# First stage of a metaformer kernel: the reciprocal standard deviations go to DRAM as all 32 rows and come back by one transfer of 128 partitions per norm

## The chip, the cores and the metric

The kernel runs on one core of a Trainium2 chip. The metric is the device time of one execution in microseconds (us).

## What is computed

The input x has the shape (2, 64, 256, 256): 2 images, 64 channels, 65,536 pixels each. The reference, cut to its skeleton:

```python
x = x + _L0_conv_ref(_ln_c(x), L0_conv_kernel)                  # norm over channels, 3x3 depthwise convolution
t = _to_tokens(x)
t = t + _L0_ffn_ref(_ln_t(t), W, V, gamma, beta)                # norm over channels, W, batch norm, recurrence with sigmoid
x = _from_tokens(t, x)
x = x + _L1_conv_ref(_ln_c(x), ...)                             # norm, linear attention
t = t + _L1_ffn_ref(_ln_t(t), ...)                              # norm, experts with top-8 tokens
```

The norms take mean and variance over the 64 channels of each pixel:

```python
def _ln_c(v, eps=1e-06):
    m = jnp.mean(v, axis=1, keepdims=True)
    s = jnp.var(v, axis=1, keepdims=True)
    return (v - m) / jnp.sqrt(s + eps)
```

The first stage of the kernel holds the first norm, the convolution with its addition (giving x1), the second norm, the product with W (giving u) and the sums for the batch norm. The change is in this stage alone.

## The kernel before

**Tiles.** The 2 x 64 channels of the two images lie on the 128 partitions: image b on partitions 64b to 64b + 63. The pixels run along the free dimension, in 32 blocks (NBLK) of 2048 pixels (BLOCK, 8 KB per partition), each of 4 tiles of 512 pixels (TILE, TPB = 4). A block of x is 1 MB.

**Order.** Each engine has its own program, written out by hand as a loop over steps t, one tile per step. At step t an engine does the work of tile t - lag for each kind of work; the lags are constants (CENTER 5, TAPS 8, SUMS 9, FINISH 10, PROJECT 22, SCALE 23). Waits are on semaphores. A round n of statistics comes every 4 steps and serves two norms at once: the first norm of block n (l = 0) and the second norm of block n - 4 (l = 1, BEHIND = 4 rounds). There are 36 rounds; rounds 0 to 3 hold only the first norm, rounds 32 to 35 only the second.

**A round.** TensorE multiplies the tiles and their squares with stat_of, which puts the mean of image b for norm l and tile j of the block into 8 equal rows of PSUM: partitions 32j + 16l + 8b to 32j + 16l + 8b + 7. VectorE takes the squared mean away (line 623), ScalarE makes 1/sqrt by a logarithm and an exponential (lines 501, 505, 509). The result is the tile `rstd` of 128 partitions x 512: 4 tiles x 2 norms x 2 images x 8 equal copies.

**The way to the channels.** A norm needs rstd on all 64 channels of an image. SyncE does it through DRAM. `rstd_to_dram(n)` (line 360) writes one of the 8 copies: for each norm and image one transfer of 4 rows of 2 KB, 8 KB in all. `rstd_to_channels(l, k)` (line 369) waits until these have landed and reads the 8 KB row of an image back into 64 partitions, one transfer of 512 KB per image, two per norm. The second norm's wait for the written rows is left out where the first norm of the same round has waited already. The tile `rb[l]` holds two blocks; it is overwritten when VectorE has used the block two before. The profile names rb[0] and u together with x as `arena`, rb[1] as `rstd_wide`.

**SyncE's order in a step**: write rstd (t - 2), spread rstd (t - 3), store x1 (`x_scratch<-arena`, line 376), store u (`xl_scratch<-arena`, line 380), load x six tiles ahead (`arena<-in_x`, line 354). All these transfers share the queue q1. After block 27's projections SyncE also issues the loads of region 0 for the second stage (`first_regions`, line 132); region 1 follows when the last u is stored.

**Users.** VectorE multiplies the centered tile with rstd of the first norm in `norm_x` (line 594, halo rows in 591 and 593), adds taps of the convolution (line 617), and multiplies the projected tile with rstd of the second norm in `scale_wx` (line 634), which also waits for the store of u two blocks before. ScalarE makes products of taps and squares, GpSimd adds them up (lines 559, 566).

**After the stage.** The sums of u give the batch norm (line 667 on), and the second stage runs the recurrence over the regions of u (first matmuls at line 859).

Of the kernel before, what the change touches and what calls it, by code (L numbers as in the profile page):

```python
# [15 lines left out]
B, C, H, W = 2, 64, 256, 256  # L16
P = B * C
N = H * W
TILE = 512
# [49 lines left out]
def build_program(nc, x, conv_k, ffn_w, ffn_v, gamma, beta, q_w, q_b, kv_w, kv_b, proj_w, proj_b,  # L69
# [4 lines left out]
    with stack:  # L74
# [6 lines left out]
        def dram(name, shape, dt=F32):  # L81
            return nc.dram_tensor(name, shape, dt, kind="Internal").ap()
# [138 lines left out]
        with ExitStack() as ph:  # L221
# [29 lines left out]
            psw = [ph.enter_context(nc.psum_tensor(f"psw{j}", [P, TILE], F32)) for j in range(2)]  # L251
            rstd_d = [dram(f"rstd_scratch{l}", (NBLK, B, BLOCK)) for l in range(2)]

# [21 lines left out]
            STEPS_A = NT + SCALE + 6  # L275

            def round_of(l, k):
                return k + BEHIND * l
# [5 lines left out]
            def rstd_written(n):  # L284

                return rstd_out[n % 2], sum(16 * B * len(norms_in(m)) for m in range(n % 2, n + 1, 2))

# [58 lines left out]
            def _(sp):  # L346
# [9 lines left out]
                def rstd_to_dram(n):  # L356
                    sp.wait_ge(rstd_ready, n + 1)
                    for l, k in norms_in(n):
                        for b in range(B):
                            sp.dma_start(rstd_d[l][k, b, :].rearrange("(j n) -> j n", n=TILE),  # L360
                                         rstd[16 * l + 8 * b:P:32, n % 2, :]).then_inc(rstd_out[n % 2], 16)

                def rstd_to_channels(l, k):
                    if l == 0 or k >= NBLK - BEHIND:
                        sp.wait_ge(*rstd_written(round_of(l, k)))
                    if k >= 2:
                        sp.wait_ge((normed, u_ready)[l], TPB * (k - 1))
                    for b in range(B):
                        sp.dma_start(rb[l][b * C:(b + 1) * C, k % 2, :],
                                     rstd_d[l][k, b, :].partition_broadcast(C)).then_inc(rb_loaded[l][k % 2], 16)  # L370

# [205 lines left out]
            def _(dve):  # L577
                dve.wait_ge(pads_ready, 1)

                def norm_x(g):  # L580
                    k, q = g // TPB, g % RT
                    dve.wait_ge(centered, g + 1)
                    dve.wait_ge(rb_loaded[0][k % 2], 32 * (k // 2 + 1))
                    if g >= RT:
# [40 lines left out]
                def scale_wx(g):  # L625
                    k = g // TPB
                    dve.wait_ge(wx_ready, g + 1)
                    dve.wait_ge(rb_loaded[1][k % 2], 32 * (k // 2 + 1))
                    if g % TPB == 0 and 2 <= k < NBLK - 2:
# [1357 lines left out]
```

## Time and profile before

| what | value |
|---|---|
| time, median of 3 runs | 1800.78 us (1798.41 to 1800.98) |
| profiled execution | 1805.67 us |
| its span, first to last instruction | 1803.9 us |
| busy in the span | TensorE 79%, VectorE 77%, ScalarE 68%, GpSimd 77% |
| first stage | about 20 to 681 us of the span |
| transfers of rstd to DRAM in the stage | 128, 8 KB each |
| transfers of rstd to the channels in the stage | 128, 512 KB each |

The span is the time from the first to the last instruction of one profiled execution. In the rows below PE is TensorE, PEld its weight loads, DVE VectorE, ACT ScalarE, POOL GpSimd, SP SyncE, SPq what SyncE's queue issues; L369 is line 369. The DMA share is the mean busy share of the core's 16 DMA engines. Busy times are of one execution; an idle time in brackets names what ended it.

### The profile page before, as it was taken

How to read it: one execution, taken by the hardware profiler on the slowest of the kernel's cores; microseconds unless marked ns; L12 is line 12 of the kernel's file. 1: busy time of each engine (PE TensorE's matmuls, PEld its weight loads, DVE VectorE, ACT ScalarE, POOL GpSimd, SP SyncE). 2: the span in 40 equal slices, each digit the busy share in tenths (PEclk: the TensorE clock that was granted, in tenths of full speed). 3: DMA queues.
4: the chain of work that ended last, by engine and by line, in shares of the span. 5: the costliest groups of instructions: out<-in, count | busy, mean ns of one | idle time of the engine just before them, and what ended most of it. 6: DMA issues, size and time to landing. Idle time of an engine off the chain costs nothing. (4 is left out here: it accounts for less than half of the span.)

```text
span 1803.9 us, 23731 instructions
## 1 busy us (share of the span) xinstructions
PE 1430.1 (79%) x5369; PEld 589.3 (33%) x5369; DVE 1384.6 (77%) x2395; ACT 1220.0 (68%) x2320; POOL 1398.0 (77%) x1029
## 2 busy tenths in 40 slices
PE   3889999999999956999926789999999999816100
PEld 1233333333333313666613333333333333205100
DVE  1899999999999954999935469999999999941000
ACT  2678888878788755999923488898898898610000
POOL 2899999999999930588882099999999999801575
PEclk8999999999999987999976899999999999955555
DMA  4579999999999889499975258988898887660011
GB/s 128 160 211 289 276 289 275 289 278 281 288 272 289 227 278 394 162 423 425 405 290 233 48 171 267 292 291 269 287 294 272 283 294 220 205 163 7 1 2 2
DMA packets 111403, 429.77 MB, mean 238 GB/s; under 512 B 44672, under 2 KB 47648, under 8 KB 66208
## 3 DMA queue, kind: packets, MB, share of 16 engines
q1 hardware_dynamic: 91376, 423.77, 73.0%
q10 hardware_dynamic: 16432, 4.29, 1.4%
q8 instruction: 47, 0.77, 0.2%
q0 software_dynamic: 3456, 0.19, 0.2%
q14 instruction: 92, 0.75, 0.1%
HBM read 257.89 MB, written 170.01 MB: 237 GB/s over the span
## 5 line engine op out<-in xcount | busy, mean ns | idle before, releaser
L617 DVE SCALAR_TENSOR_TENSOR pst<-xn,kk,pst 128x512 f32<-128x512 f32 x448 | 336.3, 751 | 7.8 <-PE pst L449 1.6
L449 PE MATMUL pst<-xn,taps 128*128 128x512 f32 x512 | 243.8, 598 | 44.6 <-DVE acc L617 44.6
L559 POOL TENSOR_TENSOR x_and_products<-tap_products,x_and_products 128x512 f32<-128x512 f32 x192 | 245.1, 1277 | 30.1 <-ACT tap_products L527 2.7
L1528 POOL TENSOR_SCALAR exp_q<-exp_q 128x512 f32<-128x512 f32 x128 | 189.6, 1481 | 75.7 <-ACT exp_q L1479 75.7
L527 ACT ACTIVATE tap_products<-xn,kk 128x512 f32<-128x512 f32 x320 | 214.9, 710 | 28.7 <-POOL x_and_products L559 25.1
L1523 POOL TENSOR_TENSOR sq_norm<-arena 128x512 f32<-128x512 f32 x128 | 188.7, 1474 | 4.4 <-DVE arena L1575 1.7
L559 POOL TENSOR_TENSOR x_and_products<-tap_products,arena 128x512 f32<-128x512 f32 x128 | 163.5, 1277 | 22.8 <-ACT tap_products L527 22.7
L945 DVE SCALAR_TENSOR_TENSOR pss<-arena,bn,pss 128x256 f32<-128x256 f32 x324 | 149.6, 489 | 32.9 <-PE pss L859 32.5
L566 POOL TENSOR_TENSOR arena<-acc,x_and_products 128x512 f32<-128x512 f32 x128 | 163.8, 1280 | 9.1 <-DVE acc L617 8.3
L1535 POOL TENSOR_TENSOR q_z<-arena,z_inv 128x512 f32<-128x512 f32 x128 | 165.4, 1292 | 0.0
L489 ACT ACTIVATE sq<-arena 128x512 f32<-128x512 f32 x256 | 146.4, 615 | 23.6 <-DMA arena<-in_x 21.6
L449 PEld LDWEIGHTS pst<-xn,taps 128*128 128x128 f32 x512 | 93.6, 189 | 180.4 <-issue 178.9
L1412 PE MATMUL ps_denominator<-arena,dT 128*128 128x512 f32 x256 | 138.6, 623 | 9.9 <-DVE arena L1569 8.6
L464 PE MATMUL psw<-arena,wcT 128*128 128x512 f32 x256 | 133.1, 605 | 16.1 <-DVE arena L634 15.8
L1406 PE MATMUL ps_query<-arena,qcT 128*128 128x512 f32 x256 | 140.3, 632 | 4.7 <-DVE arena L1560 4.7
L1795 POOL DMA_INDIRECT out<-fin,word_of_slot x88 | 86.5, 983 | 71.7 <-DVE fin L1949 45.1
L458 PE MATMUL psc<-arena,cst 128*128 128x512 f32 x256 | 136.7, 617 | 5.5 <-DVE xn L594 5.5
L1485 ACT ACTIVATE ln_d<-ps_denominator,cols 128x512 f32<-128x512 f32 x128 | 86.9, 679 | 73.0 <-PE ps_denominator L1412 72.8
L1418 PE MATMUL ps_attended<-q_z,mT 128*128 128x512 f32 x256 | 130.9, 593 | 1.1 <-POOL q_z L1535 1.1
L1569 DVE SCALAR_TENSOR_TENSOR arena<-arena,q_bias_plus,exp_q 128x512 f32<-128x512 f32 x128 | 125.5, 980 | 1.8 <-POOL exp_q L1528 1.8
L1575 DVE SCALAR_TENSOR_TENSOR arena<-ps_attended,cols,arena 128x512 f32<-128x512 f32 x128 | 95.2, 744 | 38.8 <-PE ps_attended L1418 38.0
L894 POOL TENSOR_TENSOR x_block<-x_block,arena 128x2048 f32<-128x2048 f32 x20 | 111.1, 5556 | 15.9 <-ACT arena L886 9.7
(243 smaller groups left out, 2959.0 us busy)
## 6 DMA issues: line engine op xcount, KB each, us to landing
arena<-rstd_scratch SPq DMA_DIRECT2D x128, 512.0 KB, 8.5
x_scratch<-arena SPq DMA_DIRECT2D x36, 1024.0 KB, 5.0
arena<-x_scratch SPq DMA_DIRECT2D x36, 1024.0 KB, 5.3
arena<-in_x SPq DMA_DIRECT2D x32, 1024.0 KB, 8.0
rstd_wide<-rstd_scratch SPq DMA_DIRECT2D x64, 512.0 KB, 13.1
xl_scratch<-arena SPq DMA_DIRECT2D x32, 1024.0 KB, 15.6
out<-arena SPq DMA_DIRECT2D x32, 1024.0 KB, 6.6
x_transposed<-x_squares SPq DMA_DIRECT2D x64, 512.0 KB, 4.4
```

Source lines behind the costliest of these rows:

```text
L449: m = pe.matmul(wide(pst[g % 2]), taps[:, n * P:(n + 1) * P], tap_rows(g, t), start=(n == 0), stop=(n == len(mine) - 1))
L489: act.activation(sq[l][:, g % TPB, :], x_tile(g), ACT.Square).then_inc(squared[l], 1)
L527: act.activation(prod[:, q % NP, :, :], tap_rows(g, t), ACT.Copy, scale=kk[:, t:t + 1]).then_inc(products, 1)
L559: pool.tensor_tensor(xr[:, g % XR, :], prod[:, q % NP, :, :].rearrange("p r w -> p (r w)"), xr[:, g % XR, :] if n else x_tile(g), ALU.add) ...
L566: pool.tensor_tensor(x_tile(g), acc[:, g % 2, :, :].rearrange("p r w -> p (r w)"), xr[:, g % XR, :], ALU.add).then_inc(x1_ready, 1)
L617: dve.scalar_tensor_tensor(out=out, in0=tap_rows(g, t), scalar=kk[:, t:t + 1], in1=wide(pst[g % 2]), op0=ALU.mult, op1=ALU.add).then_inc(a ...
L945: dve.scalar_tensor_tensor(out=ps_at(r, j), in0=u, scalar=gain_w, in1=ps_at(r, j), op0=ALU.mult, op1=ALU.add).then_inc(summed, 1)
L1406: pe.matmul(pq[g % 2][:, :], qcT[:, :], x_tile(g), start=True, stop=True).then_inc(q_ready, 1)
L1412: pe.matmul(pd[:, :], dT[:, :], qm[:, g % QSLOTS, :], start=True, stop=True).then_inc(d_ready, 1)
L1523: pool.tensor_tensor(sq[1][:, g % SQSLOTS[1], :], x_tile(g), x_tile(g), ALU.mult).then_inc(squared[1], 1)
L1528: pool.tensor_scalar(e, e, 1.0, None, ALU.min).then_inc(clipped, 1)
L1535: pool.tensor_tensor(qz[:, g % 2, :], qm[:, g % QSLOTS, :], zr[:, g % 2, :], ALU.mult).then_inc(qz_ready, 1)
```

## The change

`rstd_to_dram` writes all 32 rows of each of the 4 partition groups, so every one of the 8 copies of both norms and images: 4 transfers of 64 KB in each round, also in the rounds with a single norm (whose other rows hold no statistics that anyone reads). `rstd_to_channels` reads a norm's 16 rows (8 copies for each image) by one transfer of 1 MB into 128 partitions, each row 8 times in a row. The scratch in DRAM becomes one tensor of 36 x 32 x 2048, and the counts of the waits follow.

```diff
-            rstd_d = [dram(f"rstd_scratch{l}", (NBLK, B, BLOCK)) for l in range(2)]
...
+            rstd_d = dram("rstd_scratch", (ROUNDS, 32, BLOCK))
...
             def rstd_written(n):
 
-                return rstd_out[n % 2], sum(16 * B * len(norms_in(m)) for m in range(n % 2, n + 1, 2))
+                return rstd_out[n % 2], 16 * TPB * (n // 2 + 1)
...
                 def rstd_to_dram(n):
                     sp.wait_ge(rstd_ready, n + 1)
-                    for l, k in norms_in(n):
-                        for b in range(B):
-                            sp.dma_start(rstd_d[l][k, b, :].rearrange("(j n) -> j n", n=TILE),
-                                         rstd[16 * l + 8 * b:P:32, n % 2, :]).then_inc(rstd_out[n % 2], 16)
+                    for j in range(TPB):
+                        sp.dma_start(rstd_d[n, :, cols_of(j)],
+                                     rstd[32 * j:32 * j + 32, n % 2, :]).then_inc(rstd_out[n % 2], 16)
 
                 def rstd_to_channels(l, k):
                     if l == 0 or k >= NBLK - BEHIND:
                         sp.wait_ge(*rstd_written(round_of(l, k)))
                     if k >= 2:
                         sp.wait_ge((normed, u_ready)[l], TPB * (k - 1))
-                    for b in range(B):
-                        sp.dma_start(rb[l][b * C:(b + 1) * C, k % 2, :],
-                                     rstd_d[l][k, b, :].partition_broadcast(C)).then_inc(rb_loaded[l][k % 2], 16)
+                    rows = rstd_d[round_of(l, k), 16 * l:16 * l + 16, :]
+                    sp.dma_start(rb[l][:, k % 2, :],
+                                 rows.unsqueeze(1).to_broadcast([16, P // 16, BLOCK])).then_inc(rb_loaded[l][k % 2], 16)
...
-                    dve.wait_ge(rb_loaded[0][k % 2], 32 * (k // 2 + 1))
+                    dve.wait_ge(rb_loaded[0][k % 2], 16 * (k // 2 + 1))
...
-                    dve.wait_ge(rb_loaded[1][k % 2], 32 * (k // 2 + 1))
+                    dve.wait_ge(rb_loaded[1][k % 2], 16 * (k // 2 + 1))
```

## Rows read from the trace of the kernel before

**Rows 1.** Busy by stretch (window, its length, busy per engine), two rounds.

```profile
core 0: us, PE busy (x) PEld busy (x) DVE busy (x) ACT busy (x) POOL busy (x), PEclk, DMA share, GB/s
147.50:165.90 18.40, 16.87 (x63) 6.42 (x63) 17.81 (x32) 15.84 (x31) 17.54 (x15) 1.00 1.00 290
...
391.20:410.00 18.80, 18.03 (x66) 7.01 (x65) 18.48 (x33) 15.38 (x31) 17.58 (x15) 1.00 0.96 277
```

**Rows 2.** Groups by line, VectorE, 100 to 640: busy, mean ns | idle before <-releasers.

```profile
L617 DVE SCALAR_TENSOR_TENSOR pst<-xn,kk,pst 128x512 f32<-128x512 f32 x403 | 302.5, 751 | 5.8 <-PE pst L449 0.6
L617 DVE SCALAR_TENSOR_TENSOR acc<-xn,kk,pst 128x512 f32<-128x512 f32 x115 | 86.0, 748 | 4.1
...
L634 DVE SCALAR_TENSOR_TENSOR arena<-psw,rstd_wide 128x512 f32<-128x512 f32 x113 | 77.3, 684 | 0.4 <-DMA xl_scratch<-arena 0.3
```

**Rows 3.** Timeline, VectorE, start: start us, us, instruction, [idle before <-releaser].

```profile
43.65 1.29 DVE L594 TENSOR_TENSOR xn<-psc,arena 128x512 f32<-128x512 f32 x2 [7.60 <-DMA arena<-rstd_scratch]
```

**Rows 4.** Timeline, VectorE, end of the stage.

```profile
666.75 0.69 DVE L634 SCALAR_TENSOR_TENSOR arena<-psw,rstd_wide 128x512 f32<-128x512 f32 x1 [10.54 <-issue]
...
676.07 0.69 DVE L634 SCALAR_TENSOR_TENSOR arena<-psw,rstd_wide 128x512 f32<-128x512 f32 x1 [4.21 <-DMA rstd_wide<-rstd_scratch]
...
680.04 0.69 DVE L634 SCALAR_TENSOR_TENSOR arena<-psw,rstd_wide 128x512 f32<-128x512 f32 x1 [1.01 <-PE psw L464]
```

**Rows 5.** Busy by stretch: x load, spread, 128-partition transfers, weights into 64.

```profile
34.50:38.00 3.50, 3.50 (x8) 1.17 (x4) 0.70 (x1) 0.00 (x0) 0.00 (x0) 0.50 0.98 328
38.50:42.00 3.50, 0.49 (x1) 0.00 (x0) 0.00 (x0) 3.30 (x6) 0.00 (x0) 0.88 1.02 225
...
1606.00:1611.00 5.00, 0.00 (x0) 0.00 (x0) 2.37 (x11) 0.00 (x0) 0.00 (x0) 0.50 1.11 199
...
646.00:657.00 11.00, 8.00 (x29) 2.18 (x28) 6.26 (x16) 8.03 (x19) 1.27 (x1) 1.00 1.02 424
```

**Rows 6.** Timeline, SyncE's queue, a late round: issue us, time of issuing, transfer.

```profile
391.20 2.33 SPq L360 DMA_DIRECT2D rstd_scratch<-rstd  x4
...
395.65 1.45 SPq L369 DMA_DIRECT2D arena<-rstd_scratch  x2
...
398.42 0.59 SPq L380 DMA_DIRECT2D xl_scratch<-arena  x1
```

**Rows 7.** Timeline, SyncE's queue, start of the stage.

```profile
32.28 1.17 SPq L360 DMA_DIRECT2D rstd_scratch<-rstd  x2
33.49 0.43 SPq L354 DMA_DIRECT2D arena<-in_x  x1
34.62 1.13 SPq L369 DMA_DIRECT2D arena<-rstd_scratch  x2
```

**Rows 8.** Timeline, SyncE's queue, end of the stage.

```profile
635.70 1.07 SPq L360 DMA_DIRECT2D rstd_scratch<-rstd  x2
...
640.62 2.71 SPq L132 DMA_DIRECT2D arena<-xl_scratch  x4
650.46 1.07 SPq L360 DMA_DIRECT2D rstd_scratch<-rstd  x2
...
658.66 1.13 SPq L369 DMA_DIRECT2D rstd_wide<-rstd_scratch  x2
...
660.46 1.37 SPq L360 DMA_DIRECT2D rstd_scratch<-rstd  x2
668.39 1.12 SPq L369 DMA_DIRECT2D rstd_wide<-rstd_scratch  x2
```

**Rows 9.** Transfers, 100 to 640: count, KB each, median us from issue to landing.

```profile
xl_scratch<-arena SPq DMA_DIRECT2D x28, 1024.0 KB, 15.7
arena<-rstd_scratch SPq DMA_DIRECT2D x54, 512.0 KB, 10.2
```

**Rows 10.** Timeline, VectorE, the round after that of rows 6.

```profile
409.63 0.68 DVE L594 TENSOR_TENSOR xn<-psc,arena 128x512 f32<-128x512 f32 x1
...
415.78 0.68 DVE L634 SCALAR_TENSOR_TENSOR arena<-psw,rstd_wide 128x512 f32<-128x512 f32 x1
```

## What I predict, and how the numbers come out of the rows

> **What bounds the kernel now.** I read the busy shares by stretch first, then VectorE's groups of instructions in the first stage, then what waited for a transfer out of the rstd scratch, and last the issues of SyncE at both ends of the stage.
>
> In the middle of the first stage VectorE is busy for 18.48 of 18.80 us of a round [rows 1]. Of the 540 us from 100 to 640 it sat idle some 10 us in front of three of its groups, and only 0.9 us of that has a releaser: 0.6 us TensorE, 0.3 us the store of u [rows 2]. So VectorE sets the pace, and the spread of rstd, which this change touches, is hidden there. But the DMA engines are nearly full too: share 0.96 in a late round, 1.00 in an early one [rows 1]. Spreads of the first stage are waited for only at its ends: block 0's, 7.60 us [rows 3], the last block's, 4.21 us, and by my reading that of the block before it: the 10.54 us that are put down to nothing end when it lands [rows 4]. Between them lies only hidden work; the change must show at these two ends, or by filling the DMA engines until they set the pace.
>
> **The price of a spread.** The load of 1 MB of x in front of block 0's spread ran at 328 GB/s with its start, and stretches of loads and stores of 128 partitions at 424 GB/s; the spread behind that load, two transfers of 64 partitions out of one 8 KB row each, ran at 225 GB/s [rows 5]. For 1.05 MB that is 2.5 us at 424 and 4.7 us at 225. A load of weights into 64 partitions, whose source is not repeated, ran at 199 GB/s [rows 5], so repeating the source is not needed for the low rate.
>
> The new spread is one transfer of 128 partitions, but with 16 rows at its source, and each row's eight copies fill eight neighbouring partitions. No row of before shows this form. Its price lies between the two above: 2.5 us (2.2 us gained) and 4.7 us (nothing gained); nothing excludes a little more. I take 4.7 us, the row nearest to it: same tile, same bytes, rows read over and over. All the 424 GB/s rows have a source row of its own for each partition.
>
> **Part by part.**
>
> Writes, rounds with one norm (the first four and the last four). Line 360 issues four transfers instead of two: 2.33 us for four [rows 6] against 1.17 for two [rows 7] and 1.07 [rows 8], so the last one is out 1.0 to 1.2 us later. All that SyncE has behind it in its order (store of x1, load of x, the wait for the written rows at line 369, spread, store of u) comes 1.0 us later.
>
> Writes, rounds with two norms. Four issues before and after, so no time on SyncE. The bytes grow from 32 to 256 KB a round: 0.6 us of all DMA engines at 424 GB/s, 1.2 us at 225 GB/s, against under 0.15 us now. I take 0.65 us, because an issue takes over 0.5 us and the transfers so come one after another [rows 6]; 1.2 us stays in the range.
>
> Spread issues. One instead of two per norm: 1.45 us for two now [rows 6]. SyncE waits for ScalarE's rstd anyway before the next round, so this is worth nothing; at most the store of u goes out up to 1.2 us earlier, into a full queue.
>
> Waits on 16 instead of 32 in VectorE's order: same place, no price. ScalarE's wait before it overwrites an rstd buffer is two rounds old when it comes.
>
> *Start of the stage.* Now: two writes at 32.28, load of x at 33.49, spread at 34.62 [rows 7], first use at 43.65 [rows 3]. After: load and spread go out 1.0 us later, the load's data is still in front, so the spread lands 1.0 us later at 4.7 us a spread (at 2.5 us: 1.0 - 2.2 = 1.2 us earlier). VectorE does nothing else there and is never idle for long afterwards, so **+1.0 us** stays.
>
> *Middle.* A round has 18.80 us; 0.96 of that is 18.05 us of DMA work, and 0.65 us more makes 18.7: it still fits, barely. How late things may come: the store of u issued at 398.42 takes 15.7 us and so lands at 414.1, and VectorE overwrites that buffer at 415.78, 1.7 us of cover; the spread for VectorE's L594 goes out in two issues from 395.65 and lands 10.2 us after the second (about 396.4), at 406.6, for 409.63, 3 us of cover [rows 6, 9, 10]. In early rounds with share 1.00 there is no room, and some four of them add 0.65 us each, 2.6 us, against that cover. I take **+1.5 us** of new stalls, from 0 to 4.
>
> *End of the stage.* Here one transfer waits for the other [rows 8]. At 635.70 two sets of rows are written; at 640.62 the four loads of region 0 (4 MB, about 10 us at 424 GB/s) go out behind the spread; the writes of 650.46 have to pass all of that and let the spread go only at 658.66; its use is at 666.75 with the next writes (660.46) behind it; these let the last spread go at 668.39, whose use is at 676.07; the last tile starts at 680.04 [rows 4, 8]. After: 1.0 us by the issues at 635.70 (the engines have nothing to do then, so all behind is moved), 0.6 us by the bytes of the writes at 650.46, 0.6 us by those at 660.46, whose extra issues hide behind the store of u. Sum **+2.2 us**. If that cover were gone, 0.5 us more. All of stage two's loads and its first matmuls follow the last tile, so nothing behind takes it back.
>
> Sum: 1.0 + 1.5 + 2.2 = 4.7 us on the span of 1803.9 (1805.67 us with what lies around it). That execution is 4.9 us (0.27%) above the median of 1800.78; I put the difference on the median: 1805.5 us. With the bounds (0 to 4 in the middle, 0.5 either way at each end): 1802.5 to 1809.
>
> **Rivals.**
>
> *The spread gets the full rate* (2.5 us). Then block 0's spread lands 1.2 us earlier. At the end: first writes' issues +1.0, spread -2.2 in front of the region loads, bytes +0.6: the second spread goes out 0.6 us earlier, lands 2.8 earlier; bytes +0.6, -2.2 again: the last lands 4.4 us earlier. The middle gains nothing but the 0.3 us of [rows 2], since VectorE sets the pace. Sum -5.9: 1795 us. It decides once a spread takes under about 3.9 us: four spreads stand on the path (one at the start, three at the end), which then return the 1.0 + 2.2 us that the writes cost. For it: 64 partitions without a repeated source are just as slow [rows 5], so the 128 could be the cure. Against it: the source's 16 rows. The Trainium skill's page SBUF — State Buffer (same section) speaks for this case.
>
> *Partly relieved*: the new form lies midway between the two rates [rows 5], a spread takes 3.6 us. Four times 1.1 us off +3.2, no stalls in the middle: 1799.5 us.
>
> *The DMA engines become the bound*: writes at the half rate, 1.2 us a round on 18.05 to 18.4 gives 19.3 to 19.6 against 18.8; 0.5 us and more in some 25 rounds: 1812 to 1820 us. Against it: the writes mostly fall into the gap in which SyncE issues them.
>
> *Nothing happens* because all of it is hidden: excluded at both ends by the waits of [rows 3, 4]; it can only be a sum of opposite signs, the second rival.
>
> **How the numbers follow.** Forecast 0.58, full rate 0.22, partly relieved 0.12, DMA-bound 0.08. A measurement of this kernel tells 0.2% (3.6 us) from no change, so faster is under 1797.2 and slower over 1804.4. Of the forecast 0.38 lies above that and 0.20 below; full rate gives 0.19 faster and 0.03 same; partly relieved 0.10 same and 0.01 on either side; DMA-bound 0.08 slower. Together faster 0.20, same 0.33, slower 0.47. The range goes from 1795 (half of the full rate's case) to 1811 (leaving the DMA-bound case out); the forecast's own is 1802.5 to 1809.
>
> **What would show it.** The rate in the stretch of block 0's spread: about 225 GB/s for the forecast, near 424 for the first rival. The first L594 at 44.6 (forecast) or 42.4. The distance from line 369's issue to landing at the end. VectorE's idle time before L634 and L594 in the middle: waits on the store of u or on the spread of some tenths of a us in early rounds. The last L634 of the stage. I am wrong about the writes if line 360's four take other than 2.1 to 2.3 us in single rounds, and about the carry if stage two starts later but the span doesn't grow.

## The result and the profile after

| | before | changed |
|---|---|---|
| median | 1802.6 us (20 runs, 1798.12 to 1807.63) | 1806.98 us (20 runs, 1801.34 to 1810.12) |
| ratio, 95% interval | 1 | 1.0022 (1.0014 to 1.0031) |
| span of the profiled execution | 1803.9 us | 1805.4 us |

The change costs 4.4 us; by the interval, between 2.5 and 5.6 us (0.0014 and 0.0031 of 1802.6).

The stretch of block 0's spread in the changed kernel, and a stretch of loads and stores of 128 partitions at the end of the stage (busy by stretch; columns as in [rows 1], the last two are DMA share and GB/s), against [rows 5]:

```profile
39.50:43.00 3.50, 0.00 (x0) 0.00 (x0) 0.00 (x0) 3.42 (x7) 0.00 (x0) 0.97 0.98 225
649.00:661.00 12.00, 8.36 (x28) 2.19 (x28) 5.12 (x15) 9.31 (x21) 1.27 (x1) 1.00 1.00 407
```

One transfer of 128 partitions runs at 225 GB/s, as the two of 64 partitions did. The full rate, which loads and stores reach in the second row, did not come.

SyncE's queue and VectorE at the start of the stage, against [rows 3, 7]:

```profile
32.33 1.73 SPq L360 DMA_DIRECT2D rstd_scratch<-rstd  x4
34.10 0.43 SPq L355 DMA_DIRECT2D arena<-in_x  x1
35.39 0.59 SPq L369 DMA_DIRECT2D arena<-rstd_scratch  x1
...
44.39 1.29 DVE L594 TENSOR_TENSOR xn<-psc,arena 128x512 f32<-128x512 f32 x2 [8.29 <-DMA arena<-rstd_scratch]
```

Four writes are issued in 1.73 us where two took 1.17; the spread goes out 0.77 us later and VectorE starts 0.74 us later.

The middle: two rounds by stretch, against [rows 1], and VectorE's groups from 100 to 640 us (busy, mean ns | idle before <-releaser), against [rows 2]:

```profile
147.50:165.90 18.40, 17.01 (x63) 6.48 (x63) 18.08 (x33) 15.14 (x31) 17.54 (x15) 1.00 1.00 297
391.20:410.00 18.80, 18.04 (x66) 6.89 (x66) 18.48 (x33) 15.34 (x31) 17.70 (x15) 1.00 0.98 293
...
L617 DVE SCALAR_TENSOR_TENSOR pst<-xn,kk,pst 128x512 f32<-128x512 f32 x402 | 301.7, 750 | 6.5 <-PE pst L449 1.3
L594 DVE TENSOR_TENSOR xn<-psc,arena 128x512 f32<-128x512 f32 x113 | 77.3, 684 | 0.3 <-PE psc L458 0.3
L591 DVE TENSOR_TENSOR xn<-psc,arena 128x256 f32<-128x256 f32 x14 | 5.8, 418 | 1.0 <-DMA arena<-rstd_scratch 1.0
```

The DMA engines carry 293 to 297 GB/s instead of 277 to 290, the share in a late round goes from 0.96 to 0.98, and VectorE is as busy as before. One new wait shows: 1.0 us on the first norm's spread before a halo row.

SyncE's queue and then VectorE at the end of the stage, against [rows 4, 8]:

```profile
637.60 3.44 SPq L360 DMA_DIRECT2D rstd_scratch<-rstd  x4
...
644.27 2.26 SPq L132 DMA_DIRECT2D arena<-xl_scratch  x4
652.37 1.72 SPq L360 DMA_DIRECT2D rstd_scratch<-rstd  x4
...
663.62 0.53 SPq L369 DMA_DIRECT2D rstd_wide<-rstd_scratch  x1
...
664.83 2.47 SPq L360 DMA_DIRECT2D rstd_scratch<-rstd  x4
674.04 0.53 SPq L369 DMA_DIRECT2D rstd_wide<-rstd_scratch  x1
...
632.12 0.68 DVE L594 TENSOR_TENSOR xn<-psc,arena 128x512 f32<-128x512 f32 x1
...
671.04 0.69 DVE L634 SCALAR_TENSOR_TENSOR arena<-psw,rstd_wide 128x512 f32<-128x512 f32 x1 [12.92 <-issue]
...
681.59 0.69 DVE L634 SCALAR_TENSOR_TENSOR arena<-psw,rstd_wide 128x512 f32<-128x512 f32 x1 [5.22 <-DMA rstd_wide<-rstd_scratch]
...
686.23 0.69 DVE L634 SCALAR_TENSOR_TENSOR arena<-psw,rstd_wide 128x512 f32<-128x512 f32 x1 [1.01 <-PE psw L464]
```

The last L634 comes 6.2 us later than in [rows 4]. The last L594 stands at 630.21 in the trace of before and at 632.12 here, so 1.9 us of that are older, and the end of the stage itself, from the last L594 to the last L634, takes 54.1 us instead of 49.8: 4.3 us.

In this pair of executions some 3 us of the 6.2 then disappear in the third stage, 280 us behind the change: the load of line 1061 at 970 us still comes 5.9 us later, the write of line 1324 at 1020 us 2.7 us. TensorE in the stretch that begins with its first matmul there (line 1109), first before, then changed (busy by stretch; the column behind the five engines is the granted clock as a share of 2.4 GHz):

```profile
962.50:979.50 17.00, 14.84 (x22) 5.83 (x23) 1.97 (x4) 7.63 (x11) 0.00 (x0) 0.54 1.01 385
```

```profile
968.50:985.50 17.00, 14.56 (x35) 6.86 (x36) 4.39 (x9) 9.88 (x16) 0.00 (x0) 0.81 0.99 387
```

TensorE has been idle for 20.6 us in front of it and starts at 1.2 GHz in both. The clock granted over 17 us is 0.54 in one and 0.81 in the other: 35 matmuls are done in the changed kernel's stretch, 22 in the other. That is not the change's doing. In the twelve kernels of the table below the granted clock at that place goes from 0.50 to 1.00 between 5 and 16 us after the first matmul, and the order follows no edit. The two in which it rises last (before, and both moved with 16 rows) have the longest rest of the execution, 841.3 and 840.9 us from that matmul on; the others have 835.1 to 838.8. Single executions are so moved by some 3 us by a stage that nobody touched; the comparison therefore goes by medians, and the search for the cause by pieces of the first stage.

### The profile page after: what moved, and what is told of

It is laid out like the page before. It is cut to its first block and busy times, and to the rows that moved or that the text cites. A ratio compares the mean times of both kernels' runs of the same rounds, so it can differ in the third digit from the quotient of the medians.

```text
span 1805.4 us, 23683 instructions
## 1 busy us (share of the span) xinstructions
PE 1427.9 (79%) x5369; PEld 590.1 (33%) x5369; DVE 1384.8 (77%) x2395; ACT 1218.7 (68%) x2320; POOL 1397.8 (77%) x1029
## 5 line engine op out<-in xcount | busy, mean ns | idle before, releaser
L449 PE MATMUL pst<-xn,taps 128*128 128x512 f32 x512 | 244.7, 600 | 44.9 <-DVE acc L617 44.9
```

Source lines behind the costliest of these rows:

```text
L449: m = pe.matmul(wide(pst[g % 2]), taps[:, n * P:(n + 1) * P], tap_rows(g, t), start=(n == 0), stop=(n == len(mine) - 1))
```

## Experiments

For each kernel three lengths were read from VectorE's timeline: when the first L594 (norm of block 0) starts, the time from there to the last L594 (middle), and from there to the start of the last L634 (end). Lines are those of the change; in a kernel with other line numbers the same instruction is meant.

| kernel | first L594 | middle | end | ratio to before (95%) |
|---|---|---|---|---|
| before | 43.65 | 586.6 | 49.8 | 1 |
| changed | 44.39 | 587.7 | 54.1 | 1.0022 (1.0014 to 1.0031) |
| writes alone | 44.77 | 586.0 | 54.0 | 1.0034 (1.0022 to 1.0046) |
| issues alone | 45.95 | 585.4 | 52.1 | 1.0023 (1.0011 to 1.0035) |
| one row for 128 partitions | 42.34 | 585.3 | 50.7 | 1.0000 (0.9989 to 1.0010) |
| the same, rows shifted | 41.70 | 586.1 | 50.5 | 1.0011 (0.9998 to 1.0023) |
| two queues | 43.35 | 586.9 | 51.1 | 1.0002 (0.9988 to 1.0016) |
| 16 rows written | 43.84 | 586.0 | 50.2 | 0.9983 (0.9970 to 0.9996) |
| region 0 later | 44.21 | 586.8 | 45.8 | 0.9966 (0.9954 to 0.9978) |
| changed, region 0 later | 44.70 | 585.3 | 47.1 | 0.9977 (0.9964 to 0.9990) |
| both regions moved | 44.32 | 585.5 | 45.5 | 0.9973 (0.9958 to 0.9987) |
| both moved, 16 rows written | 43.41 | 585.5 | 44.9 | 0.9961 (0.9947 to 0.9974) |

Pairs with the same traffic at the end agree there within 0.3 us (54.1 and 54.0, 50.7 and 50.5, 45.8 and 45.5); the middle scatters by 1.4 us among kernels with the traffic of before (586.6, 586.8, 585.5) and by 2.4 us among those with the changed writes.

### One source row for all 128 partitions

```diff
-                    rows = rstd_d[round_of(l, k), 16 * l:16 * l + 16, :]
                     sp.dma_start(rb[l][:, k % 2, :],
-                                 rows.unsqueeze(1).to_broadcast([16, P // 16, BLOCK]))
+                                 rstd_d[round_of(l, k), 16 * l, :].partition_broadcast(P))
```

> The changed kernel, but each spread reads one row of the scratch 128 times (`rstd_d[round, 16 l, :]` to all 128 partitions) instead of 16 rows 8 times each. The second image's partitions so get the first image's rstd, and their values are wrong. Writes, bytes, issues and waits are those of the changed kernel; only the shape of the source differs. Theory (the split of the source over 16 rows keeps the low rate, repeating a row doesn't): the spread of block 0 runs at about 400 GB/s instead of 225, 2.5 us instead of 4.7; the first L594 of VectorE starts at about 42.2 instead of 44.4; the three spreads at the end of the stage each land 2.2 us earlier; the whole is some 6 to 9 us faster than the changed kernel, 1798 to 1801 us, ratio to the kernel before 0.997 to 0.999. Rival (a row read over and over sets the rate, whatever the number of partitions): the stretch of the spread stays at 225 GB/s, first L594 at 44.4, time as the changed kernel, ratio 1.002.

Busy by stretch, block 0's spread and the second norm's last but one:

```profile
39.00:41.00 2.00, 0.00 (x0) 0.00 (x0) 0.00 (x0) 1.43 (x3) 0.00 (x0) 0.85 0.97 410
660.00:662.00 2.00, 0.00 (x0) 0.00 (x0) 0.00 (x0) 0.00 (x0) 0.00 (x0) 0.50 1.01 221
```

Block 0's spread has 410 GB/s and the first L594 is 2.05 us earlier than in the changed kernel, as the theory said. So a row read 128 times is no obstacle, and the 16 rows of the change are what kept the low rate there. But the second norm's spread at the end of the stage, the same instruction with another row and another tile, still has 221. That is not so wherever the second norm is spread. In its first round the load of x, the first norm's spread and the second norm's are issued at 92.07, 92.87 and 93.58, with nothing behind them until 108.23, and in the 7 us in which they pass the rate is full:

```profile
96.00:103.00 7.00, 6.44 (x33) 2.31 (x26) 6.55 (x11) 4.67 (x9) 6.86 (x6) 1.00 1.02 425
```

These are 2.98 MB, the three transfers together. So the tile is not what makes the spreads at the end slow. And the whole is at the time of before, not at 0.997 to 0.999: half of my expectation failed.

### The same with the rows shifted

```diff
-            rstd_d = dram("rstd_scratch", (ROUNDS, 32, BLOCK))
+            rstd_d = dram("rstd_scratch", (32 * ROUNDS + 16, BLOCK))
...
-                        sp.dma_start(rstd_d[n, :, cols_of(j)],
+                        sp.dma_start(rstd_d[32 * n + 16:32 * n + 48, cols_of(j)],
```

> The run with one source row for 128 partitions again (the second image gets the first one's rstd, so its values are wrong), with the scratch shifted by 16 rows of 8 KB: the row of the first norm now lies where the second norm's lay within a group of 32 rows, and the other way round. In that run the first norm's spread came at the full rate (410 GB/s in the stretch of block 0's), the second norm's at the end of the stage at about 216 to 221. Theory (where in DRAM the row lies decides): the rates change places: block 0's spread 200 to 240 GB/s and first L594 near 44.4, the second norm's spreads at the end near 400 GB/s. Rival (it is the second norm's place in SyncE's queue or its tile in SBUF): block 0's stays at about 410 GB/s with the first L594 near 42.3, those at the end stay at 200 to 230. Time in both cases within 0.2% of the kernel before.

The same two stretches:

```profile
39.00:41.00 2.00, 0.00 (x0) 0.00 (x0) 0.00 (x0) 1.81 (x4) 0.00 (x0) 0.98 0.94 397
660.00:662.00 2.00, 0.00 (x0) 0.00 (x0) 0.00 (x0) 0.00 (x0) 0.00 (x0) 0.50 0.97 221
```

The rates did not change places, so the row's place in DRAM, as far as this shift moves it, is out. The tile in SBUF is out by the 425 GB/s of the single-row run. What slows the spreads at the end of the stage stays open.

### Two rows read 64 times each

```diff
-                    for b in range(B):
-                        sp.dma_start(rb[l][b * C:(b + 1) * C, k % 2, :],
-                                     rstd_d[l][k, b, :].partition_broadcast(C))
+                    sp.dma_start(rb[l][:, k % 2, :],
+                                 rstd_d[l][k, :, :].unsqueeze(1).to_broadcast([B, C, BLOCK]))
```

> The kernel before, its writes unchanged, but each norm is spread by one transfer of 128 partitions whose source is the two images' rows, each read 64 times. Theory (the transfer engines are shared out by the rows of the source, and 16 rows gave 16 engines): two rows give few engines; the stretch of block 0's spread falls far below 225 GB/s, toward 30 to 60, a spread takes 20 to 35 us, and with two spreads in a round of 18.8 us the stage gets longer by hundreds of us. Rival (any one transfer into 128 partitions is shared out alike, and only the 16 rows of the change were unlucky): the spread runs near 400 GB/s, first L594 near 41 to 42, last L634 some 6 to 8 us earlier than 680, ratio 0.996. Second rival (the copies of a row are unrolled before the sharing out, in 8 partitions an engine as in the change): 225 GB/s, ratio 1.000.

2752.91 us, ratio 1.53. A stretch of block 0's spread, and the first L593 (its use) on VectorE's timeline:

```profile
39.00:43.00 4.00, 0.00 (x0) 0.00 (x0) 0.00 (x0) 3.60 (x7) 0.00 (x0) 0.76 0.13 54
```

```profile
60.23 1.29 DVE L593 TENSOR_TENSOR xn<-psc,arena 128x512 f32<-128x512 f32 x2 [25.09 <-DMA arena<-rstd_scratch]
```

### One write of 128 partitions

```diff
-                    for j in range(TPB):
-                        sp.dma_start(rstd_d[n, :, cols_of(j)],
-                                     rstd[32 * j:32 * j + 32, n % 2, :]).then_inc(rstd_out[n % 2], 16)
+                    sp.dma_start(rstd_d[n, :, :].rearrange("q (j n) -> j q n", n=TILE),
+                                 rstd[:, n % 2, :]).then_inc(rstd_out[n % 2], 16)
```

> The changed kernel with its four writes of a round put into one transfer of all 128 partitions; the bytes stay at 256 KB a round. Theory (by my terms the bytes are 1.2 of the 2.2 us of the end and part of the middle, the issues 1.0 us at the start and 1.0 at the end): the first L594 comes at 43.0 to 43.4 instead of 44.4, the last L634 1 to 2 us earlier than 684.5, ratio to the kernel before 1.0005 to 1.0015. Rival (issues are the whole loss): ratio 0.999 to 1.000. Second rival (bytes are the whole loss): first L594 earlier, but the ratio stays at 1.002.

1840.73 us, 1.0211 (1.0185 to 1.0237): no theory expected that. Busy by stretch, while the load of x and the spread should follow:

```profile
38.00:40.50 2.50, 0.07 (x1) 0.00 (x0) 0.00 (x0) 0.00 (x0) 0.00 (x0) 0.96 0.24 93
```

The share of 0.24 is 4 of 16: the destination's first dimension is the four tiles, and by that share 64 KB stand on each of four engines ahead of their shares of x and of the spread. The first use of the spread is 46.84 instead of 44.39, and the middle takes 613.5 us instead of 587.7; from 100 to 640 us VectorE waits 8.8 us for the first norm's spread before the halo rows alone. As a test of issues against bytes it says nothing; the next two do.

### The writes alone, and the issues alone

The first has the changed kernel's writes with the reads of before:

```diff
-                    rows = rstd_d[round_of(l, k), 16 * l:16 * l + 16, :]
-                    sp.dma_start(rb[l][:, k % 2, :],
-                                 rows.unsqueeze(1).to_broadcast([16, P // 16, BLOCK]))
+                    for b in range(B):
+                        sp.dma_start(rb[l][b * C:(b + 1) * C, k % 2, :],
+                                     rstd_d[round_of(l, k), 16 * l + 8 * b, :].partition_broadcast(C))
```

> The changed kernel's writes (all 32 rows of a round, four transfers of 64 KB) with the reads of the kernel before (two spreads into 64 partitions each, out of one 8 KB row each). Theory (the writes are the whole loss, the new spread costs what the old ones cost): ratio to the kernel before 1.001 to 1.003 as the changed kernel's 1.0022; first L594 at 44.4 to 44.7; spread at 225 GB/s; at the end of the stage the last L634 between 683 and 687. Rival (the new form of spread is what costs, and the writes are hidden): ratio 1.000, first L594 near 43.7, last L634 near 680.

The second is the kernel before with two more small writes in the rounds that have one norm:

```diff
+                    if len(norms_in(n)) == 1:
+                        for b in range(B):
+                            sp.dma_start(spare_d[n, b, :].rearrange("(j n) -> j n", n=TILE),
+                                         rstd[16 * l + 8 * b:P:32, n % 2, :]).then_inc(rstd_out[n % 2], 16)
```

> The kernel before, but in the rounds with one norm (the first four and the last four) its two writes are issued twice, the second time into a scratch that nobody reads: four issues as in the changed kernel, and only 32 KB. It isolates my term for the issues: 1.0 us at the start and 1.0 at the end. Theory: the first spread is issued 0.6 to 1.0 us later than 34.62, the last L634 comes 1 to 2 us after 680.04, ratio 1.0005 to 1.0012, under half of the change's loss; the rest is then the bytes'. Rival (the issues are the whole loss): last L634 at 684 to 686, ratio 1.002. Second rival (issues are hidden at the end): last L634 at 680 to 680.6.

The last L634 of the first (line 634) and of the second (line 639):

```profile
684.81 0.69 DVE L634 SCALAR_TENSOR_TENSOR arena<-psw,rstd_wide 128x512 f32<-128x512 f32 x1 [1.01 <-PE psw L464]
```

```profile
683.50 0.69 DVE L639 SCALAR_TENSOR_TENSOR arena<-psw,rstd_wide 128x512 f32<-128x512 f32 x1 [1.01 <-PE psw L469]
```

The writes alone have the whole loss: the end takes 54.0 us against 54.1 in the changed kernel, the ratio is 1.0034, a little above the expected band, and the new spread in sum neither costs nor saves. The issues alone make the end 2.3 us longer, more than twice my term, and the time as much longer as the whole change (1.0023); the last L634 comes later than I expected from them, but short of the 684 to 686 of its rival. That ratio is not the price of the changed kernel's issues, though. The four small writes take 2.21 us at the start where the changed kernel's four take 1.73, the first spread goes out at 35.90, 1.28 us later than before instead of 0.6 to 1.0, and the first L594 stands at 45.95, later than in any kernel with the large writes: 2.3 us of this run's loss lie at the start. SyncE's queue in that kernel, the last two rounds of the stage:

```profile
651.63 1.08 SPq L361 DMA_DIRECT2D rstd_scratch<-rstd  x2
652.75 1.00 SPq L365 DMA_DIRECT2D rstd_spare<-rstd  x2
...
662.75 1.41 SPq L361 DMA_DIRECT2D rstd_scratch<-rstd  x2
664.20 2.92 SPq L365 DMA_DIRECT2D rstd_spare<-rstd  x2
671.34 1.12 SPq L374 DMA_DIRECT2D rstd_wide<-rstd_scratch  x2
```

In the last round two issues take 2.92 us, with the spread and the store of u still in the queue ahead of them. But the last of them ends at 667.12 and the spread goes out at 671.34: it waits for the written rows to land, not for the issue.

The end of the stage can be read piece by piece, from SyncE's queue and VectorE's timeline. The three late writes are those that [rows 8] shows at 635.70, 650.46 and 660.46; the second stands 14.8 us behind the first in all six kernels, however long the first is issued.

| piece of the end, us | before | changed | writes alone | issues alone | one row | rows shifted |
|---|---|---|---|---|---|---|
| last L594 to the first late write | 5.49 | 5.48 | 5.49 | 5.48 | 5.48 | 5.48 |
| from there to the store of x1 behind it | 1.17 | 3.54 | 3.44 | 2.24 | 1.83 | 1.84 |
| to the last spread but one | 21.79 | 22.48 | 22.81 | 21.85 | 22.66 | 22.94 |
| to the last spread | 9.73 | 10.42 | 10.23 | 10.39 | 9.91 | 9.91 |
| to its first use | 7.68 | 7.55 | 7.42 | 7.53 | 6.58 | 6.35 |
| to the last L634 | 3.97 | 4.64 | 4.64 | 4.63 | 4.28 | 3.96 |

The second row is issuing, and all that stands behind it in SyncE's order, the 4 MB too, moves by it: two more issues of large writes cost 0.66 us (one row, rows shifted), two of small ones 1.07. In the changed kernel and with the writes alone one issue takes some 1.7 and 1.6 us on top. The third row is 0.7 to 1.15 us longer in all four kernels with the large writes and 0.06 with the issues alone: this is what the bytes cost. The fourth grows by 0.66 us with the issues alone, by 0.7 and 0.5 with the change and the writes alone, and by 0.2 with one row, so the bytes add nothing there that shows. The last row is TensorE's work on the last four tiles, before which it has waited 3.8 us in the trace of before and 3.9 in the changed kernel's (busy by stretch, in this order):

```profile
676.90:680.00 3.10, 3.08 (x4) 0.84 (x4) 1.18 (x4) 2.07 (x6) 0.00 (x0) 0.61 0.77 322
```

```profile
682.40:686.20 3.80, 3.75 (x4) 1.18 (x4) 1.20 (x4) 2.09 (x6) 0.00 (x0) 0.50 0.81 343
```

Its granted clock was 0.61 in the trace of before and 0.50, 1.2 GHz, in the other. Nine of the twelve kernels have 4.63 or 4.64 us in this row, with and without the large writes; before is the exception, so these 0.67 us are hardly the change's.

The long issue stands in the first of the three late rounds: line 360 takes 3.44 us in the changed kernel and 3.32 us with the writes alone, where four issues take 1.72 to 1.74 us in most rounds. The DMA packets from 637 to 640 us in the changed kernel, while the long issue runs (queue and kind: packets, MB, share of 16 engines):

```profile
q1 hardware_dynamic: 47, 0.07, 9.4%
q8 instruction: 1, 0.02, 3.3%
```

One packet of instructions falls into that stretch, and one into the long issue with the writes alone (636 to 639 us there). With region 0 later (below) there is none in it, and the same four take 1.74 us. The long issues of the middle, 2.92 us at 299.00 and 2.87 us at 468.39, have an instruction packet on q8 beside them too. Outside the last round, where the queue is full, all 13 single issues of over 1 us in the five kernels with writes of 64 KB have one. Beside the small writes of before such packets hold nothing up: one starts at 335.5 and one at 598.6, and the four issues take 2.11 us there as in most rounds. That the fetch holds the larger writes' issue up is the likely reading, not proven, and in how many executions it falls on the first late round a single profiled one does not tell.

### Region 0 behind the last spread

On the kernel before, and on the changed kernel:

```diff
-                    if t == NT - 1 - TPB * RBLK + PROJECT + 2:
+                    if t == TPB * (ROUNDS - 1) + 3:
                         first_regions(0)
```

> The kernel before, with one edit: the four loads of region 0 for stage two (4 MB) are issued behind the last spread of rstd instead of in front of the last two. Theory (at the end of the stage one small transfer waits for another, and the 4 MB in the queues ahead of them are most of that wait): the idle time of 10.54 us before L634 falls to 2 to 4 us, the last L634 comes at 670 to 674 instead of 680, and the ratio is 0.995 to 0.997. Rival (stage two then waits for its region, so the time only moves): the last L634 is earlier, but stage two's first matmul still stands near 689, ratio 1.000.

> The changed kernel with the one edit of the run before it: the four loads of region 0 (4 MB) behind the last spread. That edit alone took the kernel before to 0.9966. Theory (what the changed kernel loses at the end of the stage, 4.3 us, is lost because its larger writes have to pass the 4 MB): with the 4 MB gone, the change costs only the start (0.7 us), the middle (1.3 us) and its issues at the end (about 1 us), so 2.5 to 3.5 us over the kernel before with the same edit: ratio 0.998 to 0.9985. Rival (the writes cost the same at the end whatever stands in front): 5 us and more over it, ratio 0.9995 to 1.0005.

VectorE's timeline, kernel before with the edit, then the changed kernel with it:

```profile
661.72 0.69 DVE L634 SCALAR_TENSOR_TENSOR arena<-psw,rstd_wide 128x512 f32<-128x512 f32 x1 [4.69 <-issue]
...
676.84 0.69 DVE L634 SCALAR_TENSOR_TENSOR arena<-psw,rstd_wide 128x512 f32<-128x512 f32 x1 [1.01 <-PE psw L464]
...
680.36 0.42 DVE L667 TENSOR_REDUCE bn<-sums 128x2 f32<-128x256 f32 x1 [2.82 <-PEq L221]
```

```profile
661.55 0.69 DVE L634 SCALAR_TENSOR_TENSOR arena<-psw,rstd_wide 128x512 f32<-128x512 f32 x1 [5.53 <-issue]
...
677.11 0.69 DVE L634 SCALAR_TENSOR_TENSOR arena<-psw,rstd_wide 128x512 f32<-128x512 f32 x1 [1.00 <-PE psw L464]
```

More than half of the idle time of 10.54 us [rows 4] was the 4 MB: 4.69 us are left, where I expected 2 to 4. The end shrinks by 4.0 us, the last L634 comes at 676.84, later than the expected 670 to 674, and the ratio is 0.9966, inside the expected band. On top of this the change costs 1.3 us of the end (47.1 against 45.8) instead of 4.3; in time it is 0.9977 against 0.9966, some 2 us with intervals that overlap, and the expected 0.998 to 0.9985 was a little high. All of the 1.3 us lies between the last late write and the last spread (7.46 us against 6.19). Of the 3.0 us that are gone 1.7 are the long issue, which is not there in this run, and 0.7 the last four tiles, which take 4.63 us in both; this leaves some 0.6 us for the theory that the writes lose their time by passing the 4 MB.

### Fewer and smaller writes, two queues, and the best of it

Only the 16 partitions that are read, in one transfer a round (kernel before otherwise):

```diff
-                    for l, k in norms_in(n):
-                        for b in range(B):
-                            sp.dma_start(rstd_d[l][k, b, :].rearrange("(j n) -> j n", n=TILE),
-                                         rstd[16 * l + 8 * b:P:32, n % 2, :]).then_inc(rstd_out[n % 2], 16)
+                    sp.dma_start(rstd_d[n, :, :].rearrange("q (j n) -> j q n", n=TILE),
+                                 rstd[0:P:8, n % 2, :]).then_inc(rstd_out[n % 2], 16)
```

> The kernel before with the writes of a round put into one transfer of only the 16 partitions that are read (two images, two norms, four tiles: 32 KB); the spreads are those of the kernel before. Theory (issues of writes stand on the path at the start and at the end, bytes of this size don't): the spread of block 0 is issued 0.6 us earlier, first L594 at 43.0 to 43.6, last L634 0.6 to 1.5 us before 680, ratio 0.999 to 0.9997. Rival (a transfer of 16 pieces lands later than two of four): ratio 1.000 to 1.001.

0.9983 (0.9970 to 0.9996), better than expected, but its trace shows no gain: first L594 at 43.84, end 50.2 us. The issue is 0.5 us shorter, and the spread goes out only 0.17 us earlier (34.45), since the written rows land later. Where the 3 us of its median come from stays open.

The second image's spread issued by ScalarE:

```diff
-                    for b in range(B):
-                        sp.dma_start(rb[l][b * C:(b + 1) * C, k % 2, :],
-                                     rstd_d[l][k, b, :].partition_broadcast(C))
+                    sp.dma_start(rb[l][0:C, k % 2, :], rstd_d[l][k, 0, :].partition_broadcast(C))
...
+                def second_image(l, k):
+                    act.wait_ge(*rstd_written(round_of(l, k)))
...
+                    act.dma_start(rb[l][C:2 * C, k % 2, :], rstd_d[l][k, 1, :].partition_broadcast(C))
```

> The kernel before, with each norm's spread for the second image issued by ScalarE's queue instead of SyncE's, one step later in ScalarE's order than the root it has just taken. Both spreads of a norm can so be under way at once, in different halves of the partitions. Theory (64 partitions take one half of the ways into SBUF, and the two halves are independent): the two spreads together run at 350 to 420 GB/s, block 0's are in 1.5 to 2.2 us earlier, first L594 at 41.5 to 42.2, last L634 some 3 to 5 us before 680, ratio 0.997 to 0.998. Rival (a row of 8 KB read 64 times is served no faster from two queues): rate 225 GB/s, first L594 near 43.7. Second rival (ScalarE waits for the landing of the writes and passes it on): the middle of the stage gets longer, round period over 18.8 us, ratio above 1.000.

Block 0's spread:

```profile
39.00:41.00 2.00, 1.75 (x4) 0.50 (x2) 0.00 (x0) 1.97 (x4) 0.00 (x0) 0.84 1.03 295
```

295 GB/s with both halves under way, between the theory's 350 and the rival's 225; the first L594 gains 0.3 us, the end loses 1.2 us, the time is that of before. Whether the gain in rate comes from the two halves or from the two queues was not told apart; in this kernel it is not worth a wait on ScalarE.

Both regions moved, and then the 16 rows on top:

```diff
                     if (k := block_at(t, SCALE + TPB)) is not None:
+                        if k == NBLK - 1:
+                            first_regions(1)
                         store_u(k)
...
-                    if t == NT - 1 - TPB * RBLK + PROJECT + 2:
+                    if t == TPB * (ROUNDS - 1) + 3:
                         first_regions(0)
-                first_regions(1)
```

> The kernel before with region 0's loads behind the last spread, as in the earlier run (0.9966), and region 1's four loads issued ahead of the last store of u instead of behind it. Theory (between the stages VectorE waits for SyncE's last issues: 4.08 us before L667 in the kernel before, 2.82 with region 0 moved): this wait falls to 1 to 1.8 us, stage two starts 1 to 1.8 us earlier than in that run, ratio 0.9955 to 0.9962. Rival (SyncE then waits longer for the right to overwrite x, so the issues only change places): the wait stays at 2.8 us and the ratio at 0.9966.

> The same as the run beside it, with the writes of a round in one transfer of the 16 partitions that are read (that alone took the kernel before to 0.9983, though its trace showed nothing earlier than 0.1 us at the start of stage two). Theory (its gain is real and adds up): 2 to 3 us under the run beside it, ratio 0.994 to 0.995. Rival (its trace is right and its 0.9983 lay at the edge of what the measurement tells): same time as the run beside it, first L594 near 43.8 and the last L634 within 0.5 us of it.

VectorE's first instruction of the batch norm, in the first of the two (line 668) and in the second:

```profile
677.95 0.42 DVE L668 TENSOR_REDUCE bn<-sums 128x2 f32<-128x256 f32 x1 [1.96 <-PEq L221]
```

```profile
676.46 0.42 DVE L667 TENSOR_REDUCE bn<-sums 128x2 f32<-128x256 f32 x1 [1.96 <-PEq L221]
```

The wait between the stages falls from 2.82 to 1.96 us, just short of the expected 1.8, and stage two starts 2.4 us earlier than with region 0 alone, but the time doesn't follow: 0.9973 against 0.9966, with intervals that overlap, and not the expected 0.9955 to 0.9962. All three together give 1795.05 us, 0.9961 (0.9947 to 0.9974), the fastest median found here and faster than both kernels. It can't be ranked against region 0 alone, and it decides neither for the theory's 0.994 to 0.995 nor for its rival: the last L634 comes 1.5 us earlier than in the run beside it, where the rival allowed 0.5.

## Why the prediction was right in its sum, and where its parts were wrong

I predicted 1805.5 us, 4.7 us above the median shown, from three terms; the chip says 1806.98, 4.4 us above before. (The lower bound of my own range adds up to 1803.0, not 1802.5.)

*The price of a spread, 4.7 us: right*, 225 GB/s before and after. The reason held for block 0: with one source row instead of 16 the same transfer ran at 410 GB/s. What I left out is that the rate of a form is not the same at each place; at the end of the stage the second norm's spreads stay at 221 with one row too. The weights' load that I named as a witness is a poor one: its 988 packets for 1.00 MB are 1 KB each, those of the spreads 8 KB.

The Trainium skill's page DMA: Bandwidth & Descriptors (section Why a DMA increments its semaphore by 16 and not by 1) ties the number of engines to the slowest dimension of source and destination; the runs agree, 0.13 for two rows and 0.24 for four. The Trainium skill's page SBUF — State Buffer (section Door 1: The DMA port swizzle) lists 16 ports for partitions 0 to 127 against 8 for 0 to 63. Here 410 GB/s for block 0's single row fits that; 225 for 16 rows, and 221 for the single row at the end of the stage, show that 128 partitions alone do not give the full rate.

*The start, +1.0: mechanism right, size too large.* It is 0.74 us in the pair of traces. Over three executions with the writes of before (43.65, 44.21, 44.32) and three with the changed ones (44.39, 44.77, 44.70) it is 0.56 us. Four issues took 1.73 us, not the 2.33 us of [rows 6], which was a long round even before (2.11 us in most). By my own sign, 2.1 to 2.3 us, I was wrong about the writes here.

*The middle, +1.5: not borne out.* The pair of traces shows 1.2 us (587.73 against 586.56), close to the forecast by chance. Three kernels with the writes of before have 586.6, 586.8 and 585.5 us, three with the changed ones 587.7, 586.0 and 585.3: a mean difference of 0.1 us within a scatter of 1.4 and more. So far as that scatter tells, the added bytes fit into the gap that I named and then did not trust, in the rounds at share 1.00 too.

*The end, +2.2: the path was right, and one piece was missing.* It is 4.3 us in the changed kernel and 4.2 with the writes alone. By the table of its pieces the two extra issues of the first late round cost 0.66 us (I put them at 1.0), the bytes behind the 4 MB 0.69 (0.6), the last round 0.69 (0.6). I took the last round for bytes with its issues hidden behind the store of u; the issues alone cost 0.66 there, since the spread waits until the extra transfers too have landed. So far it is 2.0 us, less 0.13 for a last spread that lands a little sooner. What I had at nothing is the long issue, 1.7 us, which no row of before announced. The remaining 0.67 us are TensorE's last four tiles, hardly the change's.

Together 0.6 + 0.1 + 4.2 = 4.9 us, or 4.3 without TensorE's part, both within the 2.5 to 5.6 us of the interval. That the sum came out is in part luck: 1.4 us too much in the middle and 0.4 at the start stand against the 1.7 us of the long issue.

*That nothing behind takes it back*: the pair of profiles contradicts this, 6.2 us at the start of stage two against 1.5 us in the span. But some 3 us of that were returned by TensorE's clock in the third stage, which rises at another moment in each execution. The medians, 4.4 us apart, keep nearly all of it.

*The first rival* (full rate, 1795 us) fell, and its price was wrong as well: with the full rate at block 0 and in the second norm's first round the kernel only reached the time of before, since the three spreads at the end did not get it.

## What to carry to other kernels

At the end of a stage, where each small transfer waits for the one before, count every transfer, also those whose issue seems hidden: behind a full queue they land one after the other, and the wait stands behind the last one. Bulk loads for the next stage belong behind the last small transfer of such a chain; moving 4 MB there gave back more (0.9966) than the change cost. And before a transfer with repeated rows is written, look at the first dimension of both its sides: with 2 or 4 rows there, 2 or 4 engines worked.

## What the runs showed of the hardware

- One 8 KB row read into 128 partitions: 410 GB/s for the first norm at the start, 221 for the second at the end, 425 over the stretch with both in the second norm's first round; 16 rows read 8 times each: 225; two rows read 64 times each: 54, at a DMA share of 0.13.
- A write of 256 KB whose destination begins with a dimension of 4: DMA share 0.24, and 1.0211 in time.
- Four issues of 64 KB writes take 1.73 us in the changed kernel, or 2.58 to 3.44 us in the four rounds in which a packet of instructions stands beside one; four of 8 KB take 2.11 us, with such a packet beside them too.
- After 20.6 us of idle time TensorE started at 1.2 GHz, and over its first 17 us the granted clock was 0.54 in one execution and 0.81 in another; in twelve kernels it rose to 2.4 GHz between 5 and 16 us after the first matmul.
